# Layer-norm rows turned by DMA, the row mask moved to VectorE and the root's rounds to GpSimd, in a fused state-space, attention and feed-forward kernel

## The chip, the cores and the metric

One core of a Trainium2 chip runs the whole kernel in one launch. The metric is the device time in microseconds. The engines are TensorE (PE; its weight loads are PEld), VectorE (DVE), ScalarE (ACT), GpSimd (POOL) and SyncE (SP). Each works through its own queue in order and waits for the others by semaphores; DMA transfers are issued from SP and, in some places, ACT.

## The reference

B = 32 sequences of S = 205 rows (128 image rows, 77 text rows) with D = 1024 columns.

```python
K = einsum("chn,hnl->chl", Wc, exp(P))               # Wc from x, P from log_dt and Lambda
h = concatenate([K.real, txt], axis=1)               # (32, 205, 1024)
h = h + attention(layernorm(h)) @ wo                 # causal, 32 heads of 32, 8 key/value heads
n = layernorm(h)
h = h + n @ W_base.T + b_base + 0.5 * update(n)      # update: masked low-rank, Fourier matrix
```

`layernorm(x)` is (x - mean) / sqrt(var + 1e-5) over the 1024 columns.

## The kernel before

Five stages follow one another: `ssm` (state-space tables and products, to 198 us), `prep_qkv` (weights cut into two f16 parts), `attention` (to about 1898 us), `prep_out` and `output` (from 1986 us to the end). f32 products in attention and output are made of three f16 matmuls: high by high, high by low, low by high. The change touches `ssm` and `attention`.

`ssm` first makes four tables `tab` (128 x 2048 each: sines of turned angles times sizes) with VectorE, ScalarE and GpSimd, then loops over 16 chunks `ch` of 8 heads. In a chunk VectorE makes `es` from `tab` and the PSUM copy `ab`, GpSimd makes `u` and `u2`, VectorE adds them, and PE multiplies; heads below `SUMMED` = 2 take one matmul, the others two. A matmul with f32 operands shows as two instructions in the trace.

`attention` runs steps b = -3 to 32, and a step is a software pipeline over batches: softmax and weighting of batch b (`att`), the row maxima of b + 1 (`max`), the projections of b + 2 (`qkv`), layer norm of b + 3 (`ln`), the load of b + 4 (`load`). A step has 8 slots g, one for each key/value group. PE's order in a slot is written out by hand: scores k = 0, 1 of group g (L867), `score_rows` k = 0, 1 (mask and 4 + 2 products), the first half of the q unit, scores k = 2, `score_rows` k = 2, the second half of the q unit, `weigh` of group g - 1 (36 small matmuls, L897), and then the other units of the slot: v in slots 0 and 1, k in slots 2 and 3, `("m", 1)` in slot 0, `("m", 0)` in slot 4, and the layer-norm rows turned by PE, `("x", s - 4)`, in slots 4 to 7. Units take the two banks `psJ` in turn. ScalarE copies a filled unit to f16 (`pj_hi`), VectorE makes the low part (`pj_lo`), and PE opens unit number i only when the low part of unit i - 2 is made:

```python
if ks is FRONT:

    wait(pe, pj_lo, base + (n + which - 1))
```

ScalarE's order in a slot is three exponentials, three copies `ph`, then the copies of the slot's units in order. VectorE's order in a slot is: `take_maxes` k = 0, 1; the last unit of the slot before (`late`); `take_maxes` k = 2; the low part `pl` k = 0; `layer_norm` (slots 0 to 3); `norm` of group g - 1 (reciprocal and product); then the low parts of all units of this slot but the last. `score_rows` k waits until the maxima two banks back are taken (`s_read`), and scores k = 2 until the exponential of k = 0 is done (`exp_done`). SP restacks q and k rows between SBUF tiles with 12 DMAs for each half of each, shifts the `m` rows, loads `xin` and stores `ao`.

## Time and profile before

| | |
|---|---|
| median of 3 runs | 3081.81 us (3081.46 to 3085.93) |
| profiled execution: time, span | 3082.04 us, 3080.3 us |
| PE busy | 2781.2 us (90%) |
| VectorE busy | 1997.8 us (65%) |
| ScalarE busy | 1094.1 us (36%) |
| GpSimd busy | 1029.9 us (33%) |
| mean granted clock of TensorE | 0.965 |

Busy times are sums over the whole span. A timeline row gives the start and the length of an instruction, or of a run of like ones with its count; the bracket behind it is the idle time of the engine before it and what ended that. A matmul's length contains a pipelined tail, so the distance between two starts says what it costs the queue.

### The profile page before, as it was taken

What the parts mean: (1) busy time and instruction counts of PE and PEld (TensorE: products, weight loads), DVE (VectorE), ACT (ScalarE), POOL (GpSimd) and SP (SyncE); (2) the same over time, 40 slices, a digit from 0 to 9 for tenths busy, and PEclk for the clock granted to TensorE, in tenths of its full rate; (3) what the DMA queues carried; (4) which work ended last, traced back from release to release, by engine and by line L of the source; (5) the groups of instructions that cost most, each with busy time, mean ns of one, the idle gap of its engine ahead of it and who ended that gap; (6) DMA issues with size and microseconds to landing.
All of it is one profiled execution on the core that took longest, in us unless ns stands there. A gap on an engine that the chain in (4) does not pass through costs nothing. (4 is left out here: it accounts for less than half of the span.)

```text
span 3080.3 us, 70678 instructions
## 1 busy us (share of the span) xinstructions
PE 2781.2 (90%) x27970; PEld 2030.8 (66%) x28224; DVE 1997.8 (65%) x4642; ACT 1094.1 (36%) x2362; POOL 1029.9 (33%) x1402
## 2 busy tenths in 40 slices
PE   0847799999999999999999986699999999999999
PEld 0736698989899898989898883244444444444444
DVE  8874577787787878777787865444444444444443
ACT  3331355555555555555555565211001101100110
POOL 4631254544545454554445454011101110110110
PEclk9977899999999999999999996599999999999999
DMA  5642422222222322222222223154554455455453
GB/s 179 194 116 69 103 58 78 58 75 78 57 76 60 80 58 77 69 65 77 56 76 58 69 49 144 55 122 120 129 137 123 121 133 132 118 127 137 124 122 86
DMA packets 446040, 297.32 MB, mean 97 GB/s; under 512 B 389416, under 2 KB 407976, under 8 KB 445232
## 3 DMA queue, kind: packets, MB, share of 16 engines
q1 hardware_dynamic: 445472, 282.69, 35.7%
q10 hardware_dynamic: 240, 10.09, 1.1%
q8 instruction: 226, 3.70, 0.5%
q14 instruction: 102, 0.84, 0.1%
HBM read 116.36 MB, written 80.61 MB: 64 GB/s over the span
## 5 line engine op out<-in xcount | busy, mean ns | idle before, releaser
L693 POOL TENSOR_SCALAR_AFFINE_SELECT p<-p 128x256 f32<-128x256 f32 (+1 forms) x768 | 334.3, 437 | 762.0 <-ACT p L720 743.6
L805 DVE TENSOR_REDUCE mx<-psS 77x2 f32<-77x410 f32 (+1 forms) x768 | 449.3, 613 | 181.9 <-PE psS L912 110.7
L930 PE MATMUL psJ<-xth,qh 128*128 128x205 f16 x2048 | 522.0, 255 | 24.9 <-DVE qsl L813 24.7
L932 PE MATMUL psJ<-xth,ql 128*128 128x205 f16 x2048 | 518.4, 253 | 0.0
L931 PE MATMUL psJ<-xtl,qh 128*128 128x205 f16 x2048 | 516.5, 252 | 0.0
L720 ACT ACTIVATE p<-psT,escale 128x410 f32<-128x410 f32 (+1 forms) x768 | 410.4, 570 | 276.2 <-PE psT L870 256.8
L698 POOL TENSOR_TENSOR pl<-p,ph 128x410 f16<-128x410 f32 (+1 forms) x512 | 447.7, 894 | 102.5 <-ACT ph L727 95.7
L1257 POOL TENSOR_TENSOR hb<-h,bias_sb 128x1024 f32<-128x1024 f32 x52 | 122.5, 2355 | 962.4 <-DVE h L1293 962.4
L1271 ACT CAST xh<-xn 128x1024 f16<-128x1024 f32 x52 | 54.4, 1045 | 967.1 <-DVE xn L1302 967.1
L1332 PE MATMUL ps5O<-woh,ath 128*128 128x512 f16 x832 | 316.2, 380 | 26.3 <-DMA atl<-al 26.3
L1293 DVE SCALAR_TENSOR_TENSOR h<-ps5O,osc,h_in 128x512 f32<-128x512 f32 x104 | 78.1, 751 | 402.4 <-PE ps5O L1334 402.4
L727 ACT CAST ph<-p 128x410 f16<-128x410 f32 (+1 forms) x768 | 334.3, 500 | 6.6 <-POOL p L693 6.4
L1332 PE MATMUL ps5F<-wfh,xth 128*128 128x512 f16 x832 | 315.4, 379 | 1.2 <-DMA xtl<-xl 1.2
L1334 PE MATMUL ps5O<-woh,atl 128*128 128x512 f16 x832 | 316.2, 380 | 0.0
L1333 PE MATMUL ps5O<-wol,ath 128*128 128x512 f16 x832 | 316.2, 380 | 0.0
L1333 PE MATMUL ps5F<-wfl,xth 128*128 128x512 f16 x832 | 315.5, 379 | 0.0
L1334 PE MATMUL ps5F<-wfh,xtl 128*128 128x512 f16 x832 | 315.5, 379 | 0.0
L897 PE MATMUL psO<-vh,ph 128*128 128x33 f16 (+1 forms) x3072 | 261.4, 178 | 6.9 <-issue 5.1
L897 PE MATMUL psO<-vh,pl 128*128 128x33 f16 (+1 forms) x3072 | 260.4, 178 | 0.0
L897 PE MATMUL psO<-vl,ph 128*128 128x33 f16 (+1 forms) x3072 | 260.4, 178 | 0.0
L897 PEld LDWEIGHTS psO<-vh,ph 128*128 128x128 f16 (+1 forms) x3072 | 245.2, 97 | 9.8 <-issue 9.5
L897 PEld LDWEIGHTS psO<-vl,ph 128*128 128x128 f16 (+1 forms) x3072 | 240.7, 97 | 0.0
(227 smaller groups left out, 5906.9 us busy)
## 6 DMA issues: line engine op xcount, KB each, us to landing
a_in<-acat SPq DMA_DIRECT2D x52, 512.0 KB, 3.8
h_in<-hcat SPq DMA_DIRECT2D x52, 512.0 KB, 4.7
qst<-qsh SPq DMA_DIRECT2D x512, 51.2 KB, 2.1
out<-y SPq DMA_DIRECT2D x51, 512.0 KB, 3.1
hcat<-ob SPq DMA_DIRECT2D x64, 256.0 KB, 4.0
xin<-hcat SPq DMA_DIRECT2D x32, 512.0 KB
acat<-ao SPq DMA_DIRECT2D x32, 512.0 KB
qst<-qsl SPq DMA_DIRECT2D x256, 51.2 KB, 2.1
```

Of the source, the lines that this page charges most:

```text
L693: pool.affine_select(out=v, in_=v, compare_op=ALU.is_ge, fill=0.0, base=0, pattern=[[0, v.shape[1]], [1, w]], channel_multiplier=-1).then_ ...
L698: pool.tensor_tensor(view(pl, g % 2, k), view(p32, g % 2, k), view(ph, g % 2, k), ALU.subtract).then_inc(lo_pool, 1)
L720: act.activation(view(p32, g % 2, k), ps_view(psT[(g + k) % 2], k), ACT.Exp, scale=(escale[:, 0:1] if k < 2 else escale[0:TXT, 0:1])).then ...
L727: act.copy(view(ph, g % 2, k), view(p32, g % 2, k)).then_inc(hi_done, 1)
L805: dve.tensor_reduce(dst, v, AX.X, ALU.max).then_inc(s_read, 1)
L897: m = pe.matmul(o[:, t, r, :], p, v[0:T[j], j, g, :], start=n == 0, stop=n == len(list_) - 1)
L930: pe.matmul(ps[:, 0:S], wh[:, k, c], xth[:, par, k, :], start=k == 0, stop=False)
L931: pe.matmul(ps[:, 0:S], wh[:, k, c], xtl[:, par, k, :], start=False, stop=False)
L932: m = pe.matmul(ps[:, 0:S], wl[:, k, c], xth[:, par, k, :], start=False, stop=k == KC - 1)
L1332: pe.matmul(ps[h][:], th[:, k, :], wh[:, k, c], start=k == 0, stop=False)
L1333: pe.matmul(ps[h][:], th[:, k, :], wl[:, k, c], start=False, stop=False)
L1334: m = pe.matmul(ps[h][:], tl[:, k, :], wh[:, k, c], start=False, stop=k == KC - 1)
```

## The change

In `ssm`, GpSimd no longer takes part in the tables. ScalarE makes the sizes `size` and `ela` with 36 activations of 128 columns whose scale is a column; VectorE finds two fractions where it found four, and ScalarE gets the cosines from absolute values; VectorE makes all four products of `tab` and `size`. All 8 heads of a chunk take two matmuls, and VectorE no longer adds the first two.

In `attention`, the `x` units are gone: VectorE makes the first guess of the root (`rsqrt_guess`, 3 instructions), GpSimd the rounds (`scale_rows`, 13 instructions, in slot 3 between its selects and its subtractions), ScalarE centres and scales a row tile into `xfh` at the end of slots 4 and 5 (`high_part`), VectorE makes `xfl` in slots 4 and 5 ahead of `norm` (`low_part`), and SP turns the four tiles by DMA at the end of its step (`turn`). PE waits for `xt_in` at the start of each step. The mask of the image rows is no longer multiplied in by PE; `take_maxes` k = 0 has four `tensor_tensor_reduce` of 128 columns that add the mask and take the maximum. The load of `xin` and the store of `ao`, now in halves, are issued by ScalarE, in slots 2 and 6. SP restacks k ahead of q. `norm` has two instructions where it had four.

```diff
-            pool.wait_ge(ab_ok, 1)
-            for k in range(2):
-                pool.tensor_tensor(size[:, k], per_row(a[:]), per_step(iqr[:, k, :]), ALU.mult).then_inc(size_arg, 1)
-            pool.wait_ge(size_ok, 1)
-            for t in range(2):
-                pool.wait_ge(sine_ok, t + 1)
-                pool.tensor_tensor(tab[:, t], tab[:, t], size[:, 0], ALU.mult).then_inc(tab_ab, 1)
...
+            act.wait_ge(ab_ok, 1)
+            for k in range(2):
+                for r in range(LR):
+                    m = act.activation(size[:, k, :, r], a[:], ACT.Exp, scale=iqr[:, k, r:r + 1])
+                m.then_inc(size_ok, 1)
+            for la in range(LA):
+                m = act.activation(ela[:, la, :], a[:], ACT.Exp, scale=ila[:, la:la + 1])
+            m.then_inc(la_exp_ok, 1)
             act.wait_ge(args_ok, 1)
             act.activation(ex[:], args[:, 0].rearrange("p k h -> p (k h)"), ACT.Exp).then_inc(waves_ok, 1)
             act.activation(th[:], args[:, 0].rearrange("p k h -> p (k h)"), ACT.Tanh, scale=0.5).then_inc(waves_ok, 1)
-            for t in range(4):
-                act.wait_ge(base_ok, t // 2 + 1)
-                act.activation(turned[:, t], bases[t // 2], ACT.Identity, bias=phase[:, t:t + 1]).then_inc(turned_ok, 1)
+            act.wait_ge(turns_ok, 1)
+            act.activation(trig[:], turns[:], ACT.Sin, scale=TWO_PI).then_inc(waves_ok, 1)
             act.wait_ge(la_ok, 1)
-            act.activation(ela[:], fla[:, 0], ACT.Exp).then_inc(la_exp_ok, 1)
-            act.wait_ge(size_arg, 2)
-            act.activation(size, size, ACT.Exp).then_inc(size_ok, 1)
-            act.activation(trig[:], turns[:], ACT.Sin, scale=TWO_PI).then_inc(waves_ok, 1)
-            act.wait_ge(la_ok, 2)
...
+            act.wait_ge(frac_ok, 1)
+            act.activation(turned[:, 1], turned[:, 0], ACT.Abs, scale=-1.0, bias=phase[:, 0:1]).then_inc(far_ok, 1)
+            act.activation(tab[:, 1], turned[:, 0], ACT.Sin, scale=-TWO_PI, bias=lag[:, 0:1]).then_inc(sine_ok, 1)
+            act.wait_ge(far_ok, 1)
+            act.activation(tab[:, 0], turned[:, 1], ACT.Sin, scale=-TWO_PI, bias=quarter[:, 0:1]).then_inc(sine_ok, 1)
+            act.wait_ge(frac_ok, 2)
+            act.activation(turned[:, 3], turned[:, 2], ACT.Abs).then_inc(far_ok, 1)
+            act.activation(tab[:, 3], turned[:, 2], ACT.Sin, scale=TWO_PI).then_inc(sine_ok, 1)
+            act.wait_ge(far_ok, 2)
+            act.activation(tab[:, 2], turned[:, 3], ACT.Sin, scale=-TWO_PI, bias=quarter[:, 0:1]).then_inc(sine_ok, 1)
...
-            dve.tensor_tensor(fla[:, 0], a[:].unsqueeze(1).broadcast_to([P, LA, H]), v, ALU.mult).then_inc(la_ok, 1)
...
-            for t in range(4):
-                dve.wait_ge(turned_ok, t + 1)
-                chain(dve.tensor_scalar(tab[:, t], turned[:, t], ROUND, ROUND, ALU.add, ALU.subtract))
-                dve.tensor_tensor(turned[:, t], turned[:, t], tab[:, t], ALU.subtract).then_inc(frac_ok, 1)
+            for k in range(2):
+                m = dve.tensor_tensor(bases[k], per_row(f[:]), per_step(iqr[:, k, :]), ALU.mult)
+            chain(m)
+            chain(dve.tensor_scalar(tab[:, 0], base, phase[:, 0:1], ROUND, ALU.add, ALU.add))
+            dve.scalar_tensor_tensor(turned[:, 0], tab[:, 0], ROUND, base, ALU.subtract,
+                                     ALU.subtract).then_inc(frac_ok, 1)
+            chain(dve.tensor_scalar(tab[:, 2], base2, ROUND, None, ALU.add))
+            dve.scalar_tensor_tensor(turned[:, 2], tab[:, 2], ROUND, base2, ALU.subtract,
+                                     ALU.subtract).then_inc(frac_ok, 1)
...
-            dve.wait_ge(size_ok, 1)
-            for t in (2, 3):
-                dve.wait_ge(sine_ok, t + 1)
-                dve.tensor_tensor(tab[:, t], tab[:, t], size[:, 1], ALU.mult).then_inc(tab_cd, 1)
-            dve.wait_ge(tab_cd, 2)
+            dve.wait_ge(size_ok, 2)
+            dve.wait_ge(sine_ok, 4)
+            for t in range(4):
+                dve.tensor_tensor(tab[:, t], tab[:, t], size[:, t // 2], ALU.mult).then_inc(tab_ok, 1)
+            dve.wait_ge(tab_ok, 4)
...
-                    m = dve.tensor_tensor(es[:, ch % 2, k].rearrange("p h (q r) -> p h q r", r=LR), fast, slow, ALU.mult)
-                chain(m)
-                dve.tensor_tensor(es[:, ch % 2, 0, 0:SUMMED], es[:, ch % 2, 0, 0:SUMMED],
-                                  es[:, ch % 2, 1, 0:SUMMED], ALU.add).then_inc(e_ok, 1)
+                    dve.tensor_tensor(es[:, ch % 2, k].rearrange("p h (q r) -> p h q r", r=LR), fast, slow,
+                                      ALU.mult).then_inc(e_ok, 1)
...
-                    last = 0 if j < SUMMED else 1
-                    for k in range(last + 1):
+                    for k in range(2):
                         m = pe.matmul(ps[n % 4][:, j % 2, :], u[:, ch % 2, j].rearrange("p a c -> p (a c)"),
-                                      es[:, ch % 2, k, j, :], start=k == 0, stop=k == last)
+                                      es[:, ch % 2, k, j, :], start=k == 0, stop=k == 1)
...
-                if s >= 4 and has["ln"]:
-                    row.append(("x", s - 4))
...
-                if has["load"]:
-                    wait(sp, pj_filled, base)
-                    load(b + 4, par)
...
-                if has["last"]:
-                    store(b - 1, nxt)
                 if has["qkv"]:
+                    wait(sp, pj_lo, base + at(rows, "k", 0) + 1)
+                    wait(sp, st_filled, 24 * b + 12)
+                    restack(K_PARTS, kst[par], slice(0, 1), k_in[0])
                     wait(sp, pj_lo, base + at(rows, "q", 3) + 1)
-                    wait(sp, st_filled, 24 * b + 12)
                     restack(Q_PARTS, qst[par], HALVES[0], q_in[0])
...
-                if has["qkv"]:
-                    wait(sp, pj_lo, base + at(rows, "k", 0) + 1)
-                    restack(K_PARTS, kst[par], slice(0, 1), k_in[0])
+                if has["ln"]:
+                    wait(sp, pj_filled, base)
+                    for t in range(2):
+                        turn(t, nxt, b + 3)
...
+            def turn(t, to, n):
+                r, cols = ((P, slice(0, P)), (TROWS, slice(P, P + TROWS)))[t]
+                sp.wait_ge(x_hi, 2 * n + t + 1)
+                sp.dma_start_transpose(out=xth[:, to, :, cols], in_=xfh[0:r, t, :]).then_inc(xt_in[to], 16)
+                sp.wait_ge(x_lo, 2 * n + t + 1)
+                sp.dma_start_transpose(out=xtl[:, to, :, cols], in_=xfl[0:r, t, :]).then_inc(xt_in[to], 16)
...
+            def scale_rows(b):
+                pool.wait_ge(dve_ln, 9 * (b + 4))
+                rsqrt_rounds(links, pool, rs)
+                pool.tensor_scalar(nmean[:], mv[:, :, 0], -1.0, None, ALU.mult).then_inc(ln_done, 1)
...
+                    if g == 3 and has["ln"]:
+                        scale_rows(b)
                     for k in (1, 2):
                         pool.wait_ge(hi_done, 24 * b + 3 * g + k + 1)
                         pool.tensor_tensor(view(pl, g % 2, k), view(p32, g % 2, k), view(ph, g % 2, k),
...
+            def load(b, par):
+                act.dma_start(xin[:, par, 0, :], hcat[b * S:b * S + P, :]).then_inc(x_in[par], 16)
+                act.dma_start(xin[0:TXT, par, 1, :], hcat[b * S + P:b * S + S, :]).then_inc(x_in[par], 16)
+            def store(b, half):
+                c = slice(half * D // 2, (half + 1) * D // 2)
+                act.wait_ge(norm_done, 8 * b + 4 * half + 4)
+                act.dma_start(acat[b * S:b * S + P, c], ao[:, half, 0, :]).then_inc(a_out[half], 16)
+                act.dma_start(acat[b * S + P:b * S + S, c], ao[0:TXT, half, 1, :]).then_inc(a_out[half], 16)
...
+            def high_part(b, par, t):
+                r, x = T[t], xin[0:T[t], 1 - par, t, :]
+                if t == 0:
+                    act.wait_ge(ln_done, b + 4)
+                    if b >= -2:
+                        act.wait_ge(xt_in[par], 64 * ((b + 2) // 2 + 1))
+                act.activation(x, x, ACT.Identity, bias=nmean[0:r, t:t + 1]).then_inc(centred, 1)
+                act.wait_ge(centred, 2 * (b + 3) + t + 1)
+                act.activation(xfh[0:r, t, :], x, ACT.Copy, scale=rs[0:r, 3, t:t + 1]).then_inc(x_hi, 1)
...
                 for g in SLOTS:
+                    if g == 2 and has["load"]:
+                        wait(act, x_lo, 2 * (b + 3))
+                        load(b + 4, par)
+                    if g == 2 and has["last"]:
+                        store(b - 1, 1)
+                    if g == 6 and has["att"]:
+                        store(b, 0)
...
+                    if g in (4, 5) and has["ln"]:
+                        high_part(b, par, g - 4)
...
-                dve.reciprocal(rden[:, 0, :], o[:, 0, :, HD]).then_inc(rec_done, 1)
-                dve.reciprocal(rden[0:TXT, 1, :], o[0:TXT, 1, :, HD]).then_inc(rec_done, 1)
-                dve.wait_ge(rec_done, 2 * n + 2)
...
+                dve.reciprocal(rden[:], o[:, :, :, HD]).then_inc(rec_done, 1)
+                dve.wait_ge(rec_done, n + 1)
+                dst = ao[:, g // 4, :, g % 4 * P:(g % 4 + 1) * P].rearrange("p t (h d) -> p t h d", d=HD)
+                dve.tensor_tensor(dst, o[:, :, :, 0:HD], rden[:].unsqueeze(3).broadcast_to([P, 2, REP, HD]),
+                                  ALU.mult).then_inc(norm_done, 1)
...
-                elif g == 2:
+                else:
                     chain.n = 6
-                    rsqrt(dve, chain, rs, mv[:, :, 1])
-                else:
-                    chain.n = 18
-                    for t in range(2):
-                        r = T[t]
-                        dve.tensor_scalar(x[0:r, t, :], x[0:r, t, :], mv[0:r, t, 0:1],
-                                          rs[0:r, 3, t:t + 1], ALU.subtract, ALU.mult).then_inc(ln_done, 1)
-                    dve.sem_inc(dve_ln, 2)
+                    rsqrt_guess(chain, dve, rs, mv[:, :, 1])
+            def low_part(b, par, t):
+                r = T[t]
+                dve.wait_ge(x_hi, 2 * (b + 3) + t + 1)
+                dve.scalar_tensor_tensor(xfl[0:r, t, :], xin[0:r, 1 - par, t, :], rs[0:r, 3, t:t + 1], xfh[0:r, t, :],
+                                         ALU.mult, ALU.subtract).then_inc(x_lo, 1)
...
+                        for r in range(REP):
+                            m = dve.tensor_tensor_reduce(seen[:, r, :], src[:, r * P:(r + 1) * P], mask[:, 0, :], 1.0, LEAST,
+                                                         ALU.add, ALU.max, mx[:, 0, 4 * j + r:4 * j + r + 1])
+                        m.then_inc(s_read, 1)
...
-                    if has["ln"] and g < 4:
+                    if has["ln"] and g < 3:
                         layer_norm(b, par, g)
+                    if has["ln"] and g in (4, 5):
+                        low_part(b, par, g - 4)
                     if has["att"] and g:
                         norm(b, par, g - 1)
                     if has["last"] and not g:
...
-                    pe.matmul(ps[:], ident_bf[:], mask[:], start=True, stop=False, skip_group_check=True)
                     for r in range(REP):
                         m = pe.matmul(ps[:, r * P:(r + 1) * P], Q[0:STACK, 4 * j + r, 0:P], K[0:STACK, j, 0:P],
-                                      start=False, stop=r == REP - 1, skip_group_check=True)
+                                      start=True, stop=True)
...
-                else:
-                    t, half = divmod(n, 2)
-                    pe.wait_ge(ln_done, 2 * (b + 4))
-                    r = T[t]
-                    for k in range(4):
-                        c = 4 * half + k
-                        m = pe.transpose(ps[:, k * r:(k + 1) * r], xin[0:r, 1 - par, t, c * P:(c + 1) * P], ident[0:r, 0:r])
...
+                if has["qkv"]:
+                    pe.wait_ge(xt_in[par], 64 * ((b + 2) // 2 + 1))
...
+def rsqrt_rounds(chain, pool, rs):
+    v, y, t, out = (rs[:, k, :] for k in range(4))
+    for n in range(3):
+        chain(pool.tensor_tensor(t, y, y, ALU.mult))
+        chain(pool.tensor_tensor(t, t, v, ALU.mult))
+        chain(pool.tensor_scalar(t, t, -0.5, 1.5, ALU.mult, ALU.add))
+        chain(pool.tensor_tensor(out if n == 2 else y, t, y, ALU.mult))
```

## Rows read from the trace of the kernel before

**Rows 1.** Busy time in a stretch of attention: us, PE, PEld, DVE, ACT, POOL, clock.
```profile
840.00:1040.00 200.00, 190.41 (x2827) 179.40 (x2857) 157.57 (x411) 111.27 (x268) 98.50 (x161) 1.00 0.27 68
```
**Rows 2.** SyncE's timeline in attention: one issue of each step, the first and last of 27.
```profile
413.91 0.62 SPq L640 DMA_DIRECT2D qst<-mh  x1
...
1701.39 0.60 SPq L640 DMA_DIRECT2D qst<-mh  x1
```
**Rows 3.** Waits of PE from 340 to 1850 us: total, times, longest.
```profile
PE psJ L930 <- DVE qsl L813: 23.3, 29, 1.1
PE psJ L946 <- DVE qsl L813: 19.0, 29, 0.7
PE psS L912 <- DMA kst<-ksh: 16.9, 14, 7.0
```
**Rows 4.** PE's timeline, slots 4 and 5 of one step: start, length, instruction.
```profile
1020.45 0.52 PE L867 MATMUL psT<-qst,kst 98*128 98x410 f16 x2
...
1024.93 0.64 PE L954 MATMUL psJ<-ident,xin 128*128 128x128 f32 x4
1026.22 0.28 PE L946 MATMUL psJ<-ident,mx 128*16 128x128 f32 x1 [0.65 <-DVE qsl L813]
...
1026.41 0.51 PE L867 MATMUL psT<-qst,kst 98*128 98x410 f16 x2
...
1027.46 0.25 PE L930 MATMUL psJ<-xth,qh 128*128 128x205 f16 x1
```
**Rows 5.** Groups by line: busy us, mean ns | idle before.
```profile
L429 ACT ACTIVATE qh<-stage,qsc 128x1024 f16<-128x1024 f32 x8 | 8.4, 1134 | 16.1 <-DVEq L441 16.1
...
L447 DVE SCALAR_TENSOR_TENSOR ql<-stage,qsc,qh 128x1024 f16<-128x1024 f32 x8 | 9.7, 1280 | 0.0
...
L760 DVE TENSOR_TENSOR ao<-psO,rden 128x128 f32<-128x128 f32 (+1 forms) x512 | 123.7, 284 | 8.8
```
**Rows 6.** ScalarE's timeline in the same two slots.
```profile
1026.61 0.33 ACT L733 ACTIVATE mh<-psJ 16x205 f16<-16x205 f32 x1 [0.41 <-PE psJ L947]
```
**Rows 7.** VectorE's timeline in slot 4.
```profile
1025.12 0.18 DVE L754 RECIPROCAL rden<-psO 128x4 f32<-128x4 f32 x1 [0.66 <-PE psO L897]
...
1025.81 0.36 DVE L813 TENSOR_TENSOR qsl<-psJ,qsh 128x205 f16<-128x205 f32 x1
```
**Rows 8.** Stretches of 0.5 us with an idle PE ahead of attention; clock third from last.
```profile
283.00:283.50 0.50, 0.28 (x5) 0.12 (x2) 0.09 (x1) 0.45 (x2) 0.00 (x0) 1.00 0.11 26
...
286.00:286.50 0.50, 0.00 (x0) 0.00 (x0) 0.00 (x0) 0.00 (x0) 0.00 (x0) 0.85 0.08 21
...
288.00:288.50 0.50, 0.44 (x5) 0.44 (x5) 0.00 (x0) 0.00 (x0) 0.00 (x0) 0.50 0.12 26
...
293.00:293.50 0.50, 0.50 (x7) 0.46 (x6) 0.50 (x1) 0.00 (x0) 0.00 (x0) 0.82 0.11 25
```
**Rows 9.** DMA issues of the output stage: median us from issue to landing.
```profile
ath<-ah SPq DMA_TRANSPOSE x52, 5.3
...
xth<-xh SPq DMA_TRANSPOSE x52, 2.8
```
**Rows 10.** Timeline of the state-space stage, several engines.
```profile
8.26 3.61 DVE L274 TENSOR_SCALAR f<-b 128x128 f32<-128x128 f32 x1
...
11.90 7.84 DVE L276 TENSOR_TENSOR u<-f,iqr 128x2048 f32<-128x2048 f32 x2
...
28.30 2.29 DVE L298 TENSOR_TENSOR es<-es,tab 128x2048 f32<-128x2048 f32 x1
...
45.10 4.72 DVE L301 SCALAR_TENSOR_TENSOR t<-ex,th 128x256 f32<-128x256 f32 x1
...
63.89 6.83 DVE L347 TENSOR_TENSOR tab<-tab,stage 128x2048 f32<-128x2048 f32 x2
...
79.66 14.96 PE L379 MATMUL ps<-es,u 128*128 128x256 f32 x56 [79.66 <-DVE u L362]
...
102.46 6.31 PE L379 MATMUL ps<-es,u 128*128 128x256 f32 x28 [0.24 <-DVE u L362]
```

More of the change, by code:

```diff
@@ L252, in _ @@
             chain = Chain(dve, dve_c)
-            for t, (top, bottom) in enumerate(((0.25, 0.25), (0.5, 0.0), (0.25, 0.0), (0.0, 0.25))):
-                dve.memset(phase[0:N, t:t + 1], top)
-                m = dve.memset(phase[N:P, t:t + 1], bottom)
+            for half, back in ((slice(0, N), 0.0), (slice(N, P), -0.25)):
+                dve.memset(phase[half], back)
+                dve.memset(lag[half], back * TWO_PI)
+            m = dve.memset(quarter[:], 0.25 * TWO_PI)
             chain(m)
@@ L274, in _ @@
             chain(dve.tensor_scalar(f[:], b[:], tp, None, ALU.mult))
-            for k in range(2):
-                dve.tensor_tensor(bases[k], per_row(f[:]), per_step(iqr[:, k, :]), ALU.mult).then_inc(base_ok, 1)
             for k, src in enumerate((a, b)):
@@ L746, in norm @@
                 n = 8 * b + g
[L747 to L749 removed]
+                if g % 4 == 0:
+                    wait(dve, a_out[g // 4], 32 * b)
                 dve.wait_ge(av_done, n + 1)
@@ L772, in layer_norm @@
                     if g == 0:
-                        dve.wait_ge(x_in[1 - par], 16 * (b + 4 + par))
+                        dve.wait_ge(x_in[1 - par], 32 * ((b + 3) // 2 + 1))
+                        wait(dve, x_hi, 2 * (b + 3))
                     chain.n = 3 * g
```

90 lines of the change are left out of this document (43 added, 47 removed).

## Prediction

> **What bounds the kernel now.** I read the windows by stage first. In attention PE is busy 190.4 of 200 us and VectorE 157.6, ScalarE 111.3, GpSimd 98.5, the clock full [rows 1]. So attention, where the change lies, is bound by PE, and the reader is to see that VectorE stands close behind: what PE is relieved of counts only while VectorE, ScalarE and GpSimd deliver in time. Then SP's timeline gives the length of a step: the same issue comes 27 times from 413.91 to 1701.39 us, so a step lasts 1287.5 / 26 = 49.5 us [rows 2]. PE's waits say what of this is no work: 0.8 us (23.3 / 29) at one q unit, 0.65 us at the m unit, both for VectorE's low part, and 0.5 us (16.9 / 32 steps) for the restacked k [rows 3]. Last I laid out slots 4 and 5 of one step from the timelines of PE, ScalarE and VectorE [rows 4, 6, 7], for PE's order and those of the others are fixed, and the change moves work in them. The output stage is untouched.
>
> **PE's work after.** From the scores of slot 5 to its q unit pass 1.05 us, for 820 + 512 + 512 + 154 + 410 = 2408 columns [rows 4], 2.3 columns a ns; the mask's 512 columns are 0.22 us, eight times a step 1.8 us. An x unit of 128 rows is busy 0.64 us with its tail [rows 4]; two of these and two of 77 rows are at most 2.05 us, without tails some 1.6, which I take. With the old waits of 1.95 gone a step would need 49.5 - 1.8 - 1.6 - 1.95 = 44.2 us, and a plain slot 4.27 (slot 5 without the x unit: 0.84 to its q unit, then 3.43).
>
> **What replaces it in slot 4.** Time 0 is the start of PE's slot 4. PE ends the q unit at 3.36, `weigh` at 4.27, m at 4.46. The copy `mh` begins 0.39 after the first transpose of m (1026.22 to 1026.61) [rows 4, 6], at 4.66, and takes 0.24 of the queue. Now comes `high_part`: two activations of 1024 columns, the second waiting for the first. A scaled one takes 1.13 us [rows 5], so `x_hi` comes at 4.9 + 2 x 1.15 = 7.2. VectorE has stood at `low_part` since 3.9; its 1024 columns take 1.28 [rows 5], to 8.5. Behind it on VectorE stand `norm` and the low part of q4: from 1025.12 to 1025.81 plus 0.36 is 1.05 [rows 7]. It is done at 9.55. Unit q5 in slot 5 needs exactly this part: q4, m0, q5 are units i - 2, i - 1, i. PE reaches q5 at 4.46 + 0.84 = 5.3 and stands until 9.6: **4.3 us**. Before, VectorE split q4 without a wait for a later copy.
>
> **What follows in slots 5 to 7.** q5 is filled at 12.1 (2.5 for two halves and what lies between). ScalarE copies it by 12.9 and makes the second `high_part` until 15.2; `low_part` ends at 16.5, `norm` at 17.15. Only then does VectorE take the maxima of slot 6. Meanwhile PE has begun slot 6 at 13.0, stands 0.8 for the exponential of k = 0, which queues behind `high_part` (15.2 + 0.55), and then for the maxima of k = 0. These are four instructions now. The row nearest to one is the product of 128 PSUM columns, mean 284 ns [rows 5]; below, with the start of the next overlapping its end, I allow 0.2, above, with a separate write of its maximum, 0.4, and take 0.3, 1.2 us for the four, as the mean lies there. They end at 18.35, where PE without waits would have been at 15.9: **3.3 us** in all in slot 6. Slots 4 to 7 last 24.9 instead of 17.3.
>
> The Trainium skill, "VectorE: DVE Perf Modes", section "Two Vector instructions with no wait between them", says that an operation which writes out its accumulator is two instructions. No row here shows one; by it the upper end, 0.4, would stand, and the sum would be some 0.4 us a step longer.
>
> **The other terms of a step.** `low_part` reads two SBUF tiles beside GpSimd's selects; such an instruction of 256 columns took 4.72 us next to GpSimd's products where its like takes 0.42 [rows 10], so the two contend: nothing to 1.5, I take 0.5. In slot 2 ScalarE issues four DMAs ahead of its exponentials, 0.6 each by SP's issue [rows 2]; PE's scores k = 2 come 1.5 after it could have begun, so 2.4 of issue and 0.55 of exponential leave 1.0 of wait (0 to 1.8). The VectorE backlog at the next slot 0 costs 0.3. At nothing: GpSimd's 13 small instructions in slot 3 (bounded by 0.1 and 0.3 us each; the subtractions behind them are wanted by `weigh` in slot 4, some 2 us after they would end at 0.2 each; at 0.35 each this cover is gone), the shorter `norm`, and SP: 48 restacks and 4 m issues as before, less four, plus four transposes. These are issued by about 19, landing 2.8 later [rows 9], where PE wants them at 24.9. A step becomes 44.2 + 7.6 + 0.5 + 1.0 + 0.3 = 53.6 us, 4.1 more than 49.5. Steps with layer norm and softmax are b = 0 to 28: 29 x 4.1 = **+119 us**.
>
> **The clock.** PE fell idle at 283.28 and the granted clock from 2.4 to 1.2 GHz at about 286.35, 3.1 us later; work resumed at 288.0 and the full clock came back at about 293.2, after 5 us at half rate [rows 8]. The new gap of 4.3 to 4.8 us is longer than 3.1. Each fall would cost about 2.4 us of rate. One row does not say whether every gap does it; never and always (29 x 2.4 = 70) bound it, and I take a third, **+23 us**.
>
> **State-space stage.** GpSimd out of the tables: f 3.61 to 0.29, the two bases 7.84 to 4.6 and L301 4.72 to 0.42, each for contention gone [rows 10]; two of four fraction pairs (1.22 + 2.29) gone, and the third's product, 6.48, back to 2.29, make 7.0 and 4.2; against it four products instead of two, contended as 6.83 is for two, +6.9. With small ones (L289, the `es` and `u` additions of chunk 0, 3.9) the first matmul comes at 79.66 - 19 = about 60.7. ScalarE's 36 activations, 0.25 to 0.3 each, end before VectorE's chain of some 41 us needs them. In the loop a chunk's 28 instructions take 6.31 us [rows 10], 32 take 7.2; the loop ran at 6.83 from chunk to chunk by a chain through VectorE, and will be bound by PE: about +0.4 x 16 = 7. Net **-12 us** (-22 to 0).
>
> **Ramp and tail.** The first batch's rows go through `high_part`, `low_part` and a transpose before the first projection, 8 us later than PE's own turning, and two more steps without softmax have the slot-4 wait, less the k wait; +15. Steps 29 to 31 lose the mask, -3. Net **+12 us** (0 to 20).
>
> **Sum.** Against the profiled execution, 3082.04 (span 3080.3, and the median of the runs is 3081.81, the same within 0.01%): 3082 + 119 + 23 - 12 + 12 = **3224 us**.
>
> **The rivals.**
> A. PE never waits in slot 5, since VectorE reaches q4's low part in time, and the change is what PE saves: slots of 4.27, a step of 44.9, 29 x -4.6 = -133, total 2949. For it speaks that PE sets the pace today [rows 1]. Against it stands the order. It decides where the low part of q4 ends 4.3 us earlier than I have it; each us less of gap gives back 29 us, and below 4.6 us of waits a step the kernel is faster. 0.12, with what lies between it and no change.
> B. The masked maxima are dearer, 0.5 us each: slot 6's wait grows by 0.8, and VectorE, at 37 us of 44 by my count, fills nearly every slot. Some 1.5 us a step more: 3268. 0.12.
> C. The transposes come late. At the other row's 5.3 us to landing [rows 9], and issues behind the restacks, they arrive at about 27, 2 us after PE wants them: 3282. 0.08. A rule of the Trainium skill, "VectorE: DVE Perf Modes", section "The three transpose paths", speaks against the change here: a 128 x 128 tile takes 390 ns on TensorE and 1309 ns by DMA. By it the 26 tiles of a step would take 34 us one after another and the time would pass 3700. Row 9's 2.8 us for eight tiles disagrees, and I give it less than 0.01.
> My own forecast, with the clock as its open part, 3125 to 3270: 0.66. The small rest, 0.02, is no change.
>
> **How the numbers follow.** The point is the forecast's own. For eight in ten the range leaves out rival A (0.12) and the upper tails of B, C and the clock (0.08): 3100 to 3290. A kernel of this length is told from no change at about 0.2%, 6 us. Faster 0.12, same 0.02, slower 0.86.
>
> **What would show each step.** In the profile after: PE's q5 matmul (L930's successor) in slot 5 with an idle time of 4 to 5 us put down to VectorE's `qsl`, each step; a second of 2 to 3 us at `psS` in slot 6, put down to the maxima; SP's `qst<-mh` issues 53 to 54 us apart; `x_hi` 2.3 us after `mh`; the granted clock at half in some windows behind the gap; ScalarE's exponentials of slot 2 late by the four issues; the first matmul of the state-space stage near 61 us and chunks 7.2 apart. The prediction falls if q5 starts within 1 us of its scores, or if the masked maxima take under 0.15 or over 0.5 us each.

## The result, and the profile after

The changed kernel takes 3237.07 us (median of 4 runs, 3236.07 to 3237.70), the kernel before 3081.64; the ratio is 1.0519, 95% interval 1.0469 to 1.0569. The kernel is 5% slower, as forecast (3224, 3100 to 3290). The sum was right within 13 us, and that is in part luck: two of its terms were wrong in opposite directions, which the runs below take apart. Single executions of one kernel can lie in two groups 15 to 20 us apart (of 13 of the kernel before, three at 3062 to 3067 us and ten at 3079 to 3089), so differences of that size between medians of a few runs are read with care.

The window of the changed kernel that answers to [rows 1], same columns:

```profile
840.00:1040.00 200.00, 175.28 (x2525) 162.33 (x2524) 136.19 (x485) 110.44 (x244) 103.81 (x188) 0.94 0.34 81
```

PE is busy 15 us less of 200 and VectorE 21 less, and the clock is no longer full. The waits of PE from 340 to 1990 us (total, times, longest), to be held against [rows 3]:

```profile
PE psJ L975 <- DVE qsl L857: 115.7, 29, 4.0
PE psS L961 <- DVE mx L843: 57.9, 30, 2.0
PE psT L916 <- ACT p L759: 35.0, 54, 1.3
PE psT L913 <- DMA xtl<-xfl: 14.6, 1, 14.6
```

The first row is the wait of q5, 29 times 4.0 us; the second that of slot 6. SyncE's timeline gives the step. These are the issues of the m rows in slot 4 of steps 0 and 28; between them lie 28 periods, so a step is 1529.8 / 28 = 54.6 us against 49.5 [rows 2]:

```profile
399.23 0.60 SPq L639 DMA_DIRECT2D qst<-mh  x1
...
1928.99 0.60 SPq L639 DMA_DIRECT2D qst<-mh  x1
```

One step from slot 4 on, PE's timeline:

```profile
1042.78 0.52 PE L913 MATMUL psT<-qst,kst 98*128 98x410 f16 x2
...
1047.20 0.51 PE L913 MATMUL psT<-qst,kst 98*128 98x410 f16 x2
...
1052.18 0.35 PE L975 MATMUL psJ<-xth,qh 128*128 128x205 f16 x1 [3.99 <-DVE qsl L857]
...
1057.03 0.51 PE L913 MATMUL psT<-qst,kst 98*128 98x410 f16 x2
...
1059.45 0.33 PE L916 MATMUL psT<-qst,kst 98*77 98x308 f16 x1 [0.37 <-ACT p L759]
1061.78 0.23 PE L961 MATMUL psS<-mask,ident_bf 77*77 77x154 bf16 x1 [2.01 <-DVE mx L843]
...
1065.20 0.60 PE L913 MATMUL psT<-qst,kst 98*128 98x410 f16 x2
```

From one scores matmul (L913) to the next, slots 4, 5 and 6 last 4.42, 9.83 and 8.17 us. ScalarE's and VectorE's timelines say why:

```profile
1047.40 0.34 ACT L772 ACTIVATE mh<-psJ 16x205 f16<-16x205 f32 x1
1047.64 1.13 ACT L731 ACTIVATE xin<-xin,nmean 128x1024 f32<-128x1024 f32 x1
1048.80 1.15 ACT L733 ACTIVATE xfh<-xin,rs 128x1024 f16<-128x1024 f32 x1
```

```profile
1049.98 1.28 DVE L826 SCALAR_TENSOR_TENSOR xfl<-xin,rs,xfh 128x1024 f16<-128x1024 f32 x1 [3.11 <-ACT xfh L733]
1051.19 0.20 DVE L796 RECIPROCAL rden<-psO 128x8 f32<-128x8 f32 x1
1051.42 0.42 DVE L799 TENSOR_TENSOR ao<-psO,rden 128x256 f32<-128x256 f32 x1
1051.76 0.36 DVE L857 TENSOR_TENSOR qsl<-psJ,qsh 128x205 f16<-128x205 f32 x1
1052.04 0.28 DVE L843 CUSTOM_DVE_ANT_0 seen<-psS,mask 128x128 bf16<-128x128 f32 x1
1052.25 0.09 DVE L843 DVE_READ_ACCUMULATOR2_ANT mx<- 128x1 f32 x1
```

VectorE stands 3.11 us for `xfh`, then makes `xfl`, `norm` and at last q4's low part, with PE idle since 1048.2. This is the prediction's chain link by link. The windows of 1 us at the end of the gap and behind it (the clock is third from last, 0.50 being 1.2 GHz):

```profile
1051.00:1052.00 1.00, 0.00 (x0) 0.00 (x0) 0.97 (x4) 0.00 (x0) 0.91 (x2) 0.88 0.40 94
1052.00:1053.00 1.00, 0.81 (x5) 0.73 (x6) 1.00 (x10) 0.00 (x0) 0.00 (x0) 0.50 0.38 72
1053.00:1054.00 1.00, 1.00 (x8) 0.88 (x6) 0.73 (x2) 0.00 (x0) 0.00 (x0) 0.50 0.45 98
...
1055.00:1056.00 1.00, 1.00 (x12) 0.98 (x11) 0.81 (x2) 1.00 (x4) 0.50 (x1) 0.92 0.52 109
```

The clock falls at about 1051.8, 0.4 us before the gap ends, and PE works at half rate for some 3 us. Windows of 1 us over all of attention show this in every one of the 29 steps and not in a third of them: in 22 there are two falls of 3.4 us, one at the gap of slot 5 and one at that of slot 6, in the other 7 the two are one of 6.8 us. The clock is at half for 6.8 us of each step, which is 3.4 us of full rate.

Ahead of attention, the state-space stage and the start of the pipeline, timelines of VectorE, PE, GpSimd and SyncE:

```profile
42.48 15.90 DVE L351 TENSOR_TENSOR tab<-tab,stage 128x2048 f32<-128x2048 f32 x4
```

```profile
64.09 2.50 PE L380 MATMUL ps<-es,u 128*128 128x256 f32 x5 [64.09 <-DVE u L364]
...
357.54 0.87 PE L913 MATMUL psT<-qst,kst 98*128 98x410 f16 x2 [14.55 <-DMA xtl<-xfl]
```

```profile
242.52 0.18 POOL L1072 TENSOR_TENSOR rs<-rs 128x2 f32<-128x2 f32 x1 [8.68 <-issue]
```

```profile
309.50 0.60 SPq L619 DMA_DIRECT2D stage<-in_L_attn_wo  x1
...
311.65 10.50 SPq L619 DMA_DIRECT2D mk<-in_L_ffn_mask  x1
...
349.51 0.60 SPq L639 DMA_DIRECT2D qst<-mh  x1
...
354.86 1.28 SPq L647 DMA_TRANSPOSE xtl<-xfl  x1
```

The two spans differ by 3234.3 - 3080.3 = 154.0 us. Marks in the two timelines split it: the weights' preparation begins at 184.60 instead of 197.71 (-13.1); from there to the m issue of step 0 pass 214.6 instead of 189.3 (+25.4); 28 steps +143.5; the rest -1.8.

### The profile page after: what moved, and what is told of

Same layout as the page of the kernel before. It is cut to its first block and busy times, and to the rows that moved or that the text cites. A ratio compares the mean times of both kernels' runs of the same rounds, so it can differ in the third digit from the quotient of the medians.

```text
span 3234.3 us, 70940 instructions
## 1 busy us (share of the span) xinstructions
PE 2790.1 (86%) x27520; PEld 2020.6 (62%) x27520; DVE 1878.7 (58%) x5484; ACT 1189.2 (37%) x2394; POOL 1139.7 (35%) x1816
## 5 line engine op out<-in xcount | busy, mean ns | idle before, releaser
L975 PE MATMUL psJ<-xth,qh 128*128 128x205 f16 x2048 | 550.7, 269 | 200.3 <-DVE qsl L857 121.7
L700 POOL TENSOR_SCALAR_AFFINE_SELECT p<-p 128x256 f32<-128x256 f32 (+1 forms) x768 | 364.4, 484 | 719.2 <-ACT p L759 707.8
L976 PE MATMUL psJ<-xtl,qh 128*128 128x205 f16 x2048 | 549.4, 268 | 0.0
L977 PE MATMUL psJ<-xth,ql 128*128 128x205 f16 x2048 | 549.1, 268 | 0.0
L707 POOL TENSOR_TENSOR pl<-p,ph 128x410 f16<-128x410 f32 (+1 forms) x512 | 457.4, 914 | 82.5 <-ACT ph L766 82.5
L975 PEld LDWEIGHTS psJ<-xth,qh 128*128 128x128 f16 x2048 | 212.3, 104 | 216.5 <-DVE qsl L857 129.1
L849 DVE TENSOR_REDUCE mx<-psS 77x2 f32<-77x410 f32 x512 | 295.6, 577 | 83.6 <-PE psS L964 77.1
L843 DVE CUSTOM_DVE_ANT_0 seen<-psS,mask 128x128 bf16<-128x128 f32 x1024 | 235.6, 286 | 154.8 <-PE psS L957 154.1
```

Source lines behind the costliest of these rows:

```text
L700: pool.affine_select(out=v, in_=v, compare_op=ALU.is_ge, fill=0.0, base=0, pattern=[[0, v.shape[1]], [1, w]], channel_multiplier=-1).then_ ...
L707: pool.tensor_tensor(view(pl, g % 2, k), view(p32, g % 2, k), view(ph, g % 2, k), ALU.subtract).then_inc(lo_pool, 1)
L849: dve.tensor_reduce(dst, v, AX.X, ALU.max).then_inc(s_read, 1)
L975: pe.matmul(ps[:, 0:S], wh[:, k, c], xth[:, par, k, 0:S], start=k == 0, stop=False)
L976: pe.matmul(ps[:, 0:S], wh[:, k, c], xtl[:, par, k, 0:S], start=False, stop=False)
L977: m = pe.matmul(ps[:, 0:S], wl[:, k, c], xth[:, par, k, 0:S], start=False, stop=k == KC - 1)
```

## The experiments

All times are medians; the ratio is to the kernel before, on the same chip. "Step" is worked out from SyncE's m issues of slot 4 in steps 0 and 28, as above; the last column is the largest row of PE's waits from 340 us to the end of attention. Such a row can contain one long wait that stands ahead of step 0 and is paid once: 26.3 us of low_later's 73.7 and 25.7 of centre_early's 95.6 are of this kind.

| kernel | us | ratio, 95% | step | largest wait of PE |
|---|---|---|---|---|
| before | 3080 | 1 | 49.5 | `qsl` 23.3 |
| changed | 3237.07 | 1.0519 (1.0469 to 1.0569) | 54.6 | `qsl` 115.7 |
| fill_gaps | 3168.83 | 1.0288 (1.0273 to 1.0303) | 52.3 | exponentials 46.4 |
| low_last | 3133.85 | 1.0174 (1.0159 to 1.0190) | 51.1 | maxima 76.5 |
| low_later | 3117.11 | 1.0107 (1.0077 to 1.0136) | 50.9 | transposes 73.7 |
| centre_early | 3141.20 | 1.0197 (1.0182 to 1.0212) | 51.3 | transposes 95.6 |
| k_by_group_xt | 3086.51 | 1.0020 (0.9998 to 1.0043) | 49.4 | exponentials 76.8 |
| all_moves | 3105.07 | 1.0074 (1.0058 to 1.0090) | 49.9 | transposes 52.6 |
| ln_ahead | 3044.94 | 0.9897 (0.9863 to 0.9930) | 48.6 | maxima 44.7 |
| ln_ahead_dma_last | 3057.14 | 0.9937 (0.9916 to 0.9958) | 48.5 | maxima 47.2 |
| ln_ahead_dma_pe_mask | 3054.76 | 0.9927 (0.9907 to 0.9947) | 48.3 | m row 26.8, 21.2 of it once |
| weights_late | 3035.22 | 0.9856 (0.9840 to 0.9873) | 48.4 | maxima 44.3 |
| ssm_alone | 3065.21 | 0.9941 (0.9925 to 0.9956) | 49.6 | `qsl` 23.1 |
| mask_alone | 3055.73 | 0.9903 (0.9870 to 0.9936) | 48.9 | `qsl` 29.9 |

**What the clock costs: fill_gaps.** `fill(n, ...)` is n matmuls of 264 columns into `psO`, where `weigh` overwrites them.

```diff
+                    if g == 5 and has["att"] and has["ln"]:
+                        fill(30, b, par, g)
                     project(0, FRONT)
                     if has["att"]:
                         scores(b, par, g, 2)
+                    if g == 6 and has["att"] and has["ln"]:
+                        fill(15, b, par, g)
```

> The changed kernel with useless matmuls for PE in its two long waits of each step: 30 of 264 columns (about 3.3 us) ahead of q5 in slot 5 and 15 (1.65 us) ahead of score_rows k = 2 in slot 6; they write PSUM columns that weigh overwrites. Nothing else waits for anything new, so the gaps stay as long and only the granted clock can change. In the trace of the changed kernel the clock falls to half twice in each step, each time for 3.4 us, behind these two gaps. My theory: with PE busy it does not fall, and what it cost comes back: work done at half rate in 3.0 + 3.4 us of a step, so up to 3.2 us x 29 = 93 us: 3140 to 3170 us. Rival one, the size in my prediction: the clock is worth 23 us, 3214. Rival two: the clock's cost is hidden by the other engines' chain in slots 5 to 7 and the time stays within 10 us of 3237.

Measured 3168.83, in its range and far from both rivals: 68 us less, 2.3 a step. Its window of 1100 us in attention, same columns as [rows 1]:

```profile
600.00:1700.00 1100.00, 1046.13 (x15317) 969.09 (x15315) 760.80 (x2709) 637.75 (x1388) 598.92 (x1113) 1.00 0.35 81
```

The clock stays at 2.4 GHz, and useless work in a gap makes the kernel 2% faster. The clock's share of the loss is at least 68 us, three times my term. Slots 4 to 7 of this kernel last 4.42, 8.40, 7.26 and 4.24 us, 24.3 in all: this is what the order of work costs by itself, and I had 24.9.

**The order on VectorE: low_last and low_later.** In low_last the two `low_part` lines go behind the slot's splits:

```diff
-                    if has["ln"] and g in (4, 5):
-                        low_part(b, par, g - 4)
                     if has["att"] and g:
                         norm(b, par, g - 1)
...
+                    if has["ln"] and g in (4, 5):
+                        low_part(b, par, g - 4)
```

> The changed kernel with one move in VectorE's order: low_part of slots 4 and 5 stands at the end of the slot, behind norm and the low part of the q unit, instead of ahead of them. My theory: the wait of PE for VectorE's qsl in slot 5 (4.0 us in each of 29 steps, 3.4 to 4.3 of it at the one matmul) goes, but low_part still ends near 1051.2 in the step read, ahead of the maxima of slot 5, so PE then stands about 2.5 us at psS in slot 5, waiting for these; about 1.4 us a step come back, 40 us, and 10 to 50 us more if the shorter gaps let the granted clock alone: 3150 to 3200 us. Rival: the order of low_part and the q unit is the whole of the loss; all 4.0 us a step come back, 116 us, and the clock with it: under 3110 us.

In low_later they keep their place in the slot, one slot on (`g in (5, 6)`, `g - 5`).

> The changed kernel with low_part of the two row tiles one slot later, in slots 5 and 6 at the same place of the slot; high_part stays where it was. VectorE then never stands behind ScalarE's high_part. My theory: the wait at qsl in slot 5 and the one at the maxima in slot 6 both go, and what is left is ScalarE: high_part is 2.3 us at the end of slots 4 and 5 and the exponential of k = 0 queues behind it, about 1.0 us of PE's wait for ScalarE's exponential in slot 5 and in slot 6. A step of about 54.7 - 4.0 - 2.0 + 1.5 = 50.2 us, and the granted clock back at 2.4 GHz throughout (another 2.5 to 3.2 us a step): 3237 - 29 x 7 = about 3030 us, 2990 to 3080. Rival: low_part's 1.3 us has no idle time to lie in, VectorE turns into the bound of slots 5 and 6, and the gain is under half of that: over 3110 us.

PE's waits in low_last, 340 to 1890 us:

```profile
PE psS L961 <- DVE mx L843: 76.5, 60, 1.4
PE psT L916 <- ACT p L759: 66.0, 77, 1.4
```

and in low_later:

```profile
PE psT L913 <- DMA xtl<-xfl: 73.7, 29, 26.3
PE psT L916 <- ACT p L759: 73.1, 88, 1.6
PE psS L961 <- DVE mx L843: 21.4, 32, 0.9
```

In low_last the wait at `qsl` is gone and one at the maxima of slot 5 has come, as my theory said, but 1.4 us long and not 2.5; the time, 3134, lies below its range and above the rival's. In low_later the wait at `qsl` is gone and those at the maxima are down to 21.4 us, and yet only 120 of the 207 us expected came back. The time lies in the rival's range (over 3110), but not by its mechanism, since VectorE is not what PE waits for: something new ends last, the transposes. Of their 73.7 us one wait of 26.3 stands ahead of step 0; the other 28 are 1.7 us each, at the start of the step. (The expectation of k_by_group_xt, below, reads the row as 2.5 us in every step, which is wrong.)

**Less on ScalarE: centre_early.** The centring moves to slots 1 and 3 (`act.activation(x, x, ACT.Identity, scale=-1.0, bias=mv[0:r, t, 0:1])`).

> As low_later, and the first activation of high_part (taking the mean off) is made in slots 1 and 3, since it needs the mean alone and not the root; slots 4 and 5 keep one activation of 1024 columns each instead of two. (It is centred with the opposite sign and GpSimd's last round makes the root negative, so that no instruction is added.) My theory: ScalarE's exponential of k = 0 in slots 5 and 6 comes without a wait of PE, another 1.0 to 2.0 us a step against low_later: a step of 47.5 to 49 us and a time of 2960 to 3020 us, below the kernel before. Rival: the activation only moves its delay to slots 1 and 3, where PE then waits for the exponential or for the v and k units' copies: within 15 us of low_later.

Both missed: 24 us slower than low_later. The waits for the exponentials fell from 73.1 to 18.1 us, but those for the transposes rose to 95.6, in the steps from 1.7 to 2.4 us each. PE reached the start of the next step earlier and stood there; with the longer stand the clock falls in 27 places from 340 to 1890 us instead of 15.

**SyncE's queue: k_by_group_xt and all_moves.** SyncE's part of the edit; PE's `wait_ge(xt_in[par], ...)` also moves from the start of the step to the first projection.

```diff
                     wait(sp, pj_lo, base + at(rows, "k", 0) + 1)
-                    wait(sp, st_filled, 24 * b + 12)
-                    restack(K_PARTS, kst[par], slice(0, 1), k_in[0])
+                    for r in range(4):
+                        wait(sp, st_filled, 24 * b + 3 * (r + 1))
+                        restack(K_PARTS, kst[par], slice(0, 1), k_in[0], (r,))
```

> As low_later (3117 us), with two more moves against what bounds it now: PE stands 2.5 us at the start of each step for the last transpose. SyncE restacks k group by group as soon as the scores of that group are read, instead of all after group 3 is done, so its queue of 12 + 12 + 2 + 4 issues starts some 4 us earlier, and PE waits for the transposes ahead of its first projection instead of ahead of the scores of slot 0 (0.8 us of work). My theory: the wait for the transposes goes, 73.7 us of PE's time between 340 and 1890 us, and the clock's falls behind it: 3117 - 74 - 10 to 35 = about 3020 us, 3000 to 3050. Rival: SyncE only waits in another place, for the low parts of q3 and m, and the transposes come as late as before: over 3090 us.

> As k_by_group_xt, with the mean taken off in slots 1 and 3 as in centre_early (3141 us, where the wait for the transposes took 95.6 us of PE's time and those for ScalarE's exponentials 18.1 instead of 73.1 us). My theory: with the transposes early the shorter waits for the exponentials now reach the end: 40 to 55 us less than k_by_group_xt, 2960 to 3000 us. Rival: the waits for VectorE's maxima (45.1 us instead of 21.4) and the centring in slots 1 and 3 eat it: within 15 us of k_by_group_xt.

k_by_group_xt came to 3086.51, 31 us better than low_later where I had expected 97, and just below its rival's range. PE's waits, 340 to 1850 us, say why:

```profile
PE psT L915 <- DMA qst<-ml: 26.2, 2, 21.0
PE psJ L977 <- DMA xtl<-xfl: 25.5, 25, 3.6
```

Of the 73.7 us that were to go, the 26.3 ahead of step 0 have become a wait of 21.0 for the m row in the same place, and the 47.4 in the steps have become 25.5: together 27 us. all_moves came to 3105.07, 19 us worse than k_by_group_xt, so with its rival (within 15 us) exceeded. SyncE's timeline in one step of all_moves:

```profile
1030.78 0.53 SPq L595 DMA_DIRECT2D kst<-ksh  x1
...
1038.39 5.83 SPq L595 DMA_DIRECT2D qst<-qsh  x8
...
1048.81 1.26 SPq L647 DMA_TRANSPOSE xth<-xfh  x1
...
1052.79 2.24 SPq L649 DMA_TRANSPOSE xtl<-xfl  x1
1055.13 2.44 SPq L595 DMA_DIRECT2D kst<-ksh  x4
```

From 1030.78 to 1055.03 the queue has no hole: 12 + 12 + 2 restacks and four transposes are 24 us of issue, and the last transpose is issued as the next step has begun. The shorter the slots, the longer PE stands for it.

**Layer norm three slots earlier: ln_ahead.** Two parts of the edit, VectorE's order and SyncE's:

```diff
-                    if has["ln"] and g < 3:
-                        layer_norm(b, par, g)
+                    if has["load"] and g in (4, 6, 7):
+                        layer_norm(b + 4, (4, 6, 7).index(g))
...
+                    if has["ln"]:
+                        turn(0, nxt, b + 3)
                     wait(sp, pj_lo, base + at(rows, "k", 0) + 1)
...
+                    if has["ln"]:
+                        turn(1, nxt, b + 3)
                     wait(sp, pj_lo, base + at(rows, "q", 3) + 1)
```

> As all_moves (3105 us, 49.8 us a step, of which PE waits 1.8 for the last transpose, 1.5 for the masked maxima, 0.9 for the exponentials), with the layer norm three slots earlier: statistics in slots 4 and 6 and the guess in slot 7 of the step before, GpSimd's rounds in slot 0, ScalarE's centring in slots 7 and 0 and its copies in slots 1 and 2, the low parts in slots 2 and 3, and SyncE turns the first row tile ahead of the k restack, in a stretch in which its queue is idle for 8 us, and the second behind it. My theory: the step is now set by SyncE's queue, whose 24 + 2 + 4 issues from slot 3 on end only as the next step has begun; with the transposes ahead it ends about 4 us earlier, and PE's wait for them goes, and the statistics no longer meet the v units' slots: a step of 47.5 to 48.3 us, 3105 - 29 x 1.8 = about 3050 us, 3030 to 3065. Rival: the restacked k or q or m rows are wanted at the same time as the transposes and take their place as what PE waits for: over 3080 us.

3044.94 us, in the range: faster than both kernels. PE's waits:

```profile
PE psS L978 <- DVE mx L858: 44.7, 63, 1.0
PE psT L930 <- DMA qst<-ml: 35.4, 9, 26.2
PE psJ L992 <- DVE qsl L872: 27.4, 28, 1.0
PE psT L933 <- ACT p L769: 25.4, 31, 1.2
```

No wait for the transposes is left. The sum of the rows is 133 us, but 26.2 of it is one wait ahead of step 0; the rest over 29 steps is 3.7 us a step. 44.2 (the prediction's bare step) and 3.7 make 47.9, where 48.6 was measured, so 0.7 us a step is in no row shown here.

**Single terms on top: ln_ahead_dma_last, ln_ahead_dma_pe_mask, weights_late.** The first moves ScalarE's `load` to the end of slot 2 and its `store` to the ends of slots 3 and 6; the second puts the image rows' mask back on PE; the third changes one line of ln_ahead, `if b == -1:` ahead of the weights' loads to `if b == B - 1:`.

> As ln_ahead, and ScalarE issues its four DMAs not ahead of slot 2's exponentials but at the ends of slots 2 (load of xin) and 3 (store of ao), and the store of slot 6 at its end. The prediction's term for the issues ahead of the exponentials was 1.0 us a step (0 to 1.8). My theory: they cost PE 0.6 to 1.3 us a step at its scores k = 2 of slot 2, and 15 to 40 us come back against ln_ahead. Rival: slot 2 has slack since its k unit follows, and the time stays within 6 us of ln_ahead.

> As ln_ahead_dma_last, with the image rows' mask multiplied in by PE again and one reduction of 512 columns on VectorE. PE has 1.8 us a step more, VectorE some 0.3 x 8 = 2.4 us less. My theory: where PE is the bound again the mask on VectorE gains 0.6 to 1.7 us a step (0.63 when it was moved alone), so this kernel is 15 to 50 us slower than ln_ahead_dma_last. Rival: VectorE is what slots 4 to 7 wait for, and taking the mask from it makes the kernel as fast or faster.

> As ln_ahead (3045 us), and SyncE issues the next stage's weight loads (wo, the encoder, the coefficients and masks: 8 MB and more) in step 31 instead of step -1. In the traces these issues hold SyncE's queue for 24 us in step -1, and the restacks and transposes of that step stand behind them: PE then waits once, 14.6 us in the changed kernel (for xtl) and 26.2 us in ln_ahead (for the m row), where the kernel before waits 7.0 us. My theory: this one wait goes, with the clock's fall behind it, and nothing waits for the weights in the stage behind, since step 31 leaves some 30 us: 3045 - 20 to 30 = about 3020 us, 3012 to 3030. Rival: the loads now end in the next stage's way, whose first products wait for wo, and the time stays within 8 us of ln_ahead or rises.

Moving the four issues gained nothing (3057.14 against 3044.94, and the intervals overlap): slot 2 shrinks from 7.4 to 6.66 us and slot 3 grows from 6.62 to 7.24. That is the theory missed; the rival's 6 us are passed too, but ln_ahead's six runs lie at 3035 to 3037 and at 3053 to 3059, three in each, so its median is not known to 6 us. With the mask on PE or VectorE the time is the same (0.9927 and 0.9937), the rival's case. weights_late is 10 us below ln_ahead by the medians, and above its range (3012 to 3030). The same spread of ln_ahead stands in the way here: its three quickest runs are as quick as weights_late's four (3033 to 3038), and the intervals touch, so the times do not show what this edit is worth. The two traces do show its mechanism, with ln_ahead's taken in its slowest run: the one long wait, 26.2, is 5.1,

```profile
331.42 0.87 PE L930 MATMUL psT<-qst,kst 98*128 98x410 f16 x2 [5.09 <-DMA qst<-ml]
```

and the m issue of slot 4 in step 0 comes at 378.17 instead of 399.29 us.

At 3035.22 us, 1.4% under the kernel before, weights_late has the lowest median of these kernels.

**Two parts alone: ssm_alone and mask_alone.**

> The kernel before with the new state-space stage and nothing else of the change. My prediction's step for it is -12 us (-22 to 0); in the trace of the changed kernel the weights' preparation begins 13.1 us earlier (184.60 against 197.71). My theory: all of that arrives at the end, since the stages follow one another: 3066 to 3070 us, 13 us less. Rival: part of it is lost in the next stage, which waits for its weights' loads: less than 5 us gained.

> The kernel before with the image rows' mask on VectorE (four tensor_tensor_reduce of 128 columns instead of PE's mask product and one reduction of 512 columns) and nothing else of the change. My theory, the prediction's term: PE is the bound, so its 1.8 us a step (512 columns eight times) come off nearly in full, 30 steps and more, 40 to 58 us: 3025 to 3045 us, as the four masked maxima take VectorE 0.9 us where the one reduction took about 0.6. Rival: VectorE, 79% busy in attention before, passes the extra time on at the q and m units, whose low parts already come late, and the gain is under 20 us, or turned into a loss.

ssm_alone: 3065.21, 15 us off by the medians (ratio 0.9941, so 14 to 23), all of the stage's gain. mask_alone: 3055.73, 25 us off by the medians (ratio 0.9903, 20 to 40), between theory and rival. But its four runs are two at 3046 and 3048 and two at 3064 and 3065, half in each group where the kernel before has three of 13 in the lower. Group against group it is about 18 us off, the two profiled executions differ by 17, and the trace says the same: the step is 0.65 us shorter, 19 us over 29 steps, and not 1.8. That is the rival's case (under 20). From scores to scores slots 1, 2, 5 and 6 are each 0.1 to 0.2 us shorter, slots 3, 4 and 7 hardly at all, and slot 0 is 0.3 longer in the mean. Its waits of PE:

```profile
PE psJ L938 <- DVE qsl L822: 29.9, 29, 1.2
PE psS L920 <- issue: 23.4, 23, 6.6
```

What PE saves in slots 0, 3, 4 and 7 it stands for elsewhere. At `qsl` that is seen, 6.6 us more than before. What ends the unnamed 23.4 us is not; the first `psS` matmul stood before too, 16.9 us for the restacked k [rows 3], so only 6.5 of it are more. Together the two rows explain 13 of some 33 us missing.

## Why the prediction was right, and where its terms were not

- **The wait of slot 5** (4.3 us, behind `mh`, two activations, `xfl`, `norm`, q4): right. 3.99 us in the step read, 29 times; `xfh` ends 2.3 us after `mh`; and with the order changed (low_last) the wait at `qsl` is gone.
- **Slot 6** (0.8 + 2.5 = 3.3): the mechanism right, the size 0.9 too large: 0.37 for the exponential and 2.01 for the maxima in the step read. The masked maxima start 0.21 us apart, four of them 0.85 us and not 1.2. Rival B is out. The Trainium skill, "VectorE: DVE Perf Modes", section "Two Vector instructions with no wait between them", is borne out in kind: each shows as two instructions, the second 0.08 to 0.09 us long. But the second starts with the next operation's first, so it does not bring the 0.4 that I had tied to it.
- **The step without the clock** (+4.1): the step that failed in size. fill_gaps has 52.3 - 49.5 = +2.8, 29 x 2.8 = 82 us instead of 119. Slots 4 to 7 were 0.6 too dear. The rest lies in slots 0 to 3: 7.17, 6.97, 7.47 and 6.37 in the mean, 28.0 us, where 53.6 - 24.9 = 28.7 were forecast; my allowances for contention (0.5) and for a backlog (0.3) stand for as much. Contention did not come: `xfl` took 1.28 us, since GpSimd was idle when it started.
- **The clock** (a fall in a third of the steps, +23): wrong by a factor of three, and what filled the gap in the sum. I counted too few falls: the clock is at half for 6.8 us of every step, also at slot 6's shorter gap, which I had left out. And I made one too dear: 2.4 us of rate, from a fall that lasted 5 us [rows 8], where one here costs 1.7. It is 29 x 3.4 = 99 us of rate, of which fill_gaps gives back 68. That an error of 37 us in the step and one of 45 in the clock nearly cancel is luck. With the measured terms the sum is 82 + 68 - 13 + 18 = 155 us, where 155 was measured.
- **ScalarE's four DMAs** (1.0, 0 to 1.8): 2.0 us of issue, and PE stands up to 1.3; slot 2 is 1.1 longer than slot 3. Right, but ln_ahead_dma_last shows that it is not to be had back by moving them a slot.
- **GpSimd's rounds at nothing**: right. The 13 take 3.9 us in slot 3, and slot 3 has PE's shortest length of the four, 6.37.
- **The transposes** (rival C, 0.08): not in the changed kernel, where its single wait, 14.6 us, is the ramp's. But only since slots 5 and 6 were long. Once these were mended, C came: 1.7 us a step in low_later, 2.4 in centre_early (without the one long wait ahead of step 0 of each). By the mechanism of C, issues queued behind the restacks, and not by the engines' time: the four of a step land 3.7 to 4.1 us after issue. The page's list of DMA issues in the changed kernel, median us from issue to landing:

```profile
xth<-xfh SPq DMA_TRANSPOSE x64, 3.7
xtl<-xfl SPq DMA_TRANSPOSE x64, 4.1
```

  The Trainium skill, "VectorE: DVE Perf Modes", section "The three transpose paths", has 1309 ns for a 128 x 128 bf16 tile by DMA; by that, as an estimate, the eight tiles of one would take 10.5 us one after another. This case's trace does not agree.
- **Rival A** (no waits, 2949): no kernel here came near. Its bare step of 44.2 holds: the shortest length of each slot in steps 2 to 27 of any of these kernels, 7.07, 6.96, 6.40, 6.36, 4.41, 4.48, 4.24 and 4.24, add to 44.2. But the step of the best version is still 4.3 us longer, 3.4 of it in waits that its trace lists.
- **The mask at 1.8 us a step**: as PE's work right (0.22 us in each of slots 5 and 6), as time wrong: 0.65 alone (mask_alone), nothing in ln_ahead_dma_pe_mask.
- **State-space** (-12): -13.1 in the trace, and ssm_alone passes it on whole. Inside, the first matmul came at 64.09 and not 60.7, in the main since the four products took 15.9 us where I had 6.8 + 6.9, and the loop grew by some 2 and not 7.
- **Ramp and tail** (+12): +25.4 ahead of step 0 and -1.8 at the end leave, with one more step's 5.1 in it, about 18. From the start of the weights' preparation the first projection comes at 71.0 us (255.57) instead of 53.2 (250.86). About 9 of these 18 us are the rounds, `high_part`, `low_part` and the transposes (8 forecast); the others are GpSimd's 8.68 us before its first round, which I had missed. It stands there in five of the other versions too, 6.9 to 9.1 us, and why, without a releaser, stays open. The other 7.6 us are PE's waits up to step 0: about as many for DMA as before, and 12.9 instead of some 4 for VectorE, 9.9 of them slot 5's wait in three steps. The loads of the next stage's weights are no part of it, though weights_late shows that they cost: the kernel before stands behind them as well, 18.5 us where the changed one has 14.55.

```profile
338.54 0.87 PE L867 MATMUL psT<-qst,kst 98*128 98x410 f16 x2 [11.53 <-DMA qst<-ml]
346.40 0.63 PE L912 MATMUL psS<-kst,qst 96*128 96x128 f16 x4 [7.00 <-DMA kst<-ksh]
```

## What to carry to other kernels

When an order is fixed by hand on several queues, lay out the one slot that the change touches, instruction by instruction: the new work is paid where a later wait on the same queue stands behind it. After one wait is mended, read the waits again before the next step, since the work freed may only run into another queue; here VectorE ended last, then SyncE's issues beside ScalarE, then VectorE again. A gap of PE can cost its length and then the clock behind it, which a fill of useless matmuls prices in one run. And before a row of waits is divided by its count, look at its longest: one wait outside the loop can be a third of it.

## What the runs showed of the hardware

- The clock fell to half within 0.4 us of the end of PE's gaps of about 4.0 and 2.0 us (the second with one matmul of 0.33 us and a stand of 0.37 just ahead of it), for 6.8 us of every step; with 3.3 and 1.65 us of useless matmuls in the same gaps it did not fall once between 400 and 1900 us.
- The same `xfl` instruction took 1.28 us in the changed kernel, where GpSimd was idle when it started, and two of GpSimd's selects that began during it took 1.39 us together, elsewhere 0.90. In all_moves it took 2.03 and 1.99 us: it started 0.02 and 0.9 us behind a pair of GpSimd's subtractions `pl`, and these pairs took 2.68 and 3.52 us, elsewhere 1.69.
- One DMA issue on SyncE, usually 0.6 us, took 10.50 us just behind the load of `wo` and three small ones, and 11.13 us at the same place of the kernel before; everything queued behind it waited.
